# Four norm pieces over twelve tiles, and one rotated sum ahead of a power, in an AdaLN block with two local-attention layers

## The reference, cut to what matters

```python
x = states                                  # (4, 1024, 256), float32
sa, ca, ga, sb, cb, gb = modulation(c)      # six rows of 256 for each of 4 batches
h = layernorm(x) * (1 + ca) + sa
x = x + ga * attention(h)
h = layernorm(x) * (1 + cb) + sb            # this norm, of the last batch, is what the change cuts up
x = x + gb * ffn(h)                         # two layers, below

def layer(h):
    t = shift_token(h)                      # second half of the columns from the row before
    q, k, v = split(t @ wqkv)               # 8 heads of 64
    q, k = rotary(l2norm(q) * qs, l2norm(k) * ks)
    h = h + local_attention(q, k, v) @ wo   # window of 128, own block and the one before
    t = layernorm(shift_token(h)) * lg + lb
    a, g = split(t @ w1 + b1)
    return h + (a * gelu(g)) @ w2 + b2
```

## Time and profile before

| | us |
|---|---|
| median of 3 runs | 2335.64 |
| lowest and highest | 2334.77, 2335.74 |
| the profiled execution | 2336.77 |
| its span in the profile | 2335.0 |

### The profile page before, as it was taken

How to read it: one execution, slowest core, us unless ns; L and a number is a source line. 1 busy time by engine, 2 the same in 40 slices (tenths; PEclk the granted TensorE clock), 3 DMA queues, 4 the chain that set the end, 5 groups by cost and what they waited for, 6 DMA issues and landing times.

```text
span 2335.0 us, 61234 instructions
## 1 busy us (share of the span) xinstructions
PE 2249.1 (96%) x21120; PEld 1734.1 (74%) x21120; DVE 1918.6 (82%) x4512; ACT 1510.0 (65%) x2969; POOL 525.9 (23%) x637
## 2 busy tenths in 40 slices
PE   6999999999999999889999999999999999998999
PEld 4676777777777767567777777788777777776888
DVE  6999799979998999768888888567588888886776
ACT  5777577757776777447677766444476777765443
POOL 2000000000000000154555554012255555551000
PEclk9999999999999999989999999999999999999999
DMA  3100110001001100210000001000100000001110
GB/s 117 47 13 19 38 40 13 13 31 52 13 13 43 58 13 7 84 58 2 9 0 9 0 9 39 19 1 0 48 1 3 7 4 5 5 5 31 60 36 28
DMA packets 66987, 58.20 MB, mean 25 GB/s; under 512 B 4037, under 2 KB 64317, under 8 KB 66625
## 3 DMA queue, kind: packets, MB, share of 16 engines
q1 hardware_dynamic: 66880, 56.81, 7.9%
HBM read 44.21 MB, written 8.40 MB: 23 GB/s over the span
## 4 chain that ended last, share of the span: by engine, by line
PE 53%; DVE 2%; issue 1%; ACT 1%; POOL 0%; DVEq 0%; POOLq 0%; ACTq 0%
PE ly_ps L74 9%; PE ly_ps L75 9%; PE ly_ps L76 9%; PE ly_ps L1930 6%; PE ly_ps L1909 5%; PE ly_ps L1920 5%; PE ly_ps L1947 5%; PE ly_ps L1901 3%; PE ly_ps L1940 1%; PE ly_ps L1957 1%; PE ly_ps L1985 1%; PE ly_ps L1878 1%; DVE ly_masked L1598 1%; DVE ly_rope_t L1569 0%; DVE ly_rope_a L1566 0%
## 5 line engine op out<-in xcount | busy, mean ns | idle before, releaser
L610 ACT ACTIVATE at_p<-at_ps_s,at_shift 128x1024 f32<-128x1024 f32 (+3 forms) x384 | 335.5, 899 | 89.8 <-PE at_ps_s L814 48.9
L349 DVE TENSOR_TENSOR at_p_lo<-at_p,at_p_hi 128x1024 f16<-128x1024 f32 (+3 forms) x384 | 357.4, 952 | 5.5
L1371 ACT ACTIVATE ly_probs<-ly_masked,ly_small,ly_rq 128x256 f32<-128x256 f32 x512 | 301.6, 594 | 13.8 <-DVE ly_small L1601 13.8
L842 PE MATMUL at_ps_o<-at_v,at_p_hi 128*128 128x65 f16 x2304 | 238.0, 193 | 3.4 <-DVE at_p_lo L349 2.5
L842 PEld LDWEIGHTS at_ps_o<-at_v,at_p_hi 128*128 128x128 f16 x2304 | 210.6, 96 | 38.6 <-issue 25.8
L843 PE MATMUL at_ps_o<-at_v,at_p_hi 128*128 128x64 f16 x2304 | 237.1, 194 | 0.0
L1598 DVE CUSTOM_DVE_ANT_0 ly_masked<-ly_ps,ly_mask 128x256 f32<-128x256 f32 x512 | 196.1, 421 | 49.0 <-PE ly_ps L1909 36.6
L844 PE MATMUL at_ps_o<-at_v,at_p_lo 128*128 128x65 f16 x2304 | 236.0, 192 | 0.0
L1225 POOL TENSOR_TENSOR ly_rope_a<-ly_rope_a,ly_rope_t 128x512 f32<-128x512 f32 x128 | 164.2, 1283 | 318.5 <-DVE ly_rope_t L1569 318.5
L1379 ACT ACTIVATE ly_operands_plain<-ly_ps 128x512 f32<-128x512 f32 x256 | 153.3, 599 | 111.8 <-PE ly_ps L1920 103.9
L344 DVE CAST at_p_hi<-at_p 128x1024 f16<-128x1024 f32 (+3 forms) x384 | 206.8, 557 | 22.3 <-ACT at_p L610 13.5
(11 more groups left out here) (247 smaller groups left out, 6057.6 us busy)
## 6 DMA issues: line engine op xcount, KB each, us to landing
at_w_raw<-in_Wv SPq DMA_DIRECT2D x32, 128.0 KB, 2.3
at_w_raw<-in_Wq SPq DMA_DIRECT2D x32, 128.0 KB, 2.4
at_w_raw<-in_Wk SPq DMA_DIRECT2D x32, 128.0 KB, 2.4
at_xio<-in_states SPq DMA_DIRECT2D x4, 1024.0 KB, 6.7
ly_a_raw<-x SPq DMA_DIRECT2D x8, 512.0 KB, 4.4
out<-stream SPq DMA_DIRECT2D x16, 256.0 KB, 2.3
ly_shifted<-stream SPq DMA_DIRECT2D x8, 508.0 KB
x<-at_xio SPq DMA_DIRECT2D x3, 1024.0 KB, 4.4
```

The source lines that it names most:

```text
L349: dve.tensor_tensor(p_lo[u % P_RING][:, :, off:], probs[u % P_RING][:, :, off:], p_hi[u % P_RING][:, :, off:], ALU.subtract).then_inc(p_lo ...
L610: act.activation(probs[u % P_RING][:, :, off:], ps_s[u % 2][:, :, off:], ACT.Exp, bias=shift[:], scale=SCORE_SCALE).then_inc(exp_done, 1)
L842: pe.matmul(out, ph, ones_hi, start=(kt == 0 and t == 0), stop=False, skip_group_check=True)
L1371: step = act.activation(pr[:, j % 2, h, :], sm[:, j % 2, h, :], ACT.Exp, bias=small[:, j % 2, 1, h:h + 1], scale=rq[:, par, 2 * j + h:2 * ...
```

## The change

Two things change.

The norm of the last batch is done in four pieces of two tiles each (`piece(n)`), over tiles 0 to 11 of layer 0: statistics of piece n at the end of DVE's tile n (0 to 3), the variance and POOL's power at tile 4, the shift at tile 5, ACT's two instructions of a piece at the end of its tiles 6 to 9, the product of a piece (128x512) at the end of DVE's tiles 7 to 10, the sum of a piece at the end of DVE's tiles 8 to 11. For that the first twelve tiles of layer 0 (`HEAD = 12`) are straight code on DVE, ACT and POOL, and their loops run over tiles 12 to 27. PE's code, layer 1's loops and the DMAs stay.

And in front of tile 0 of both layers POOL sums the rotated queries (`add_rotated(l, 0, 0)`) ahead of the power for the query norms (`inverse_query_norms(l, 0, 0)`).

```diff
+NORM_PIECES = 4
+HEAD = 3 * NORM_PIECES
+
+def piece(n):
+    return range(n * TB // NORM_PIECES, (n + 1) * TB // NORM_PIECES)
...
# POOL, before tile 0 of layer 0 (and the same two lines of layer 1)
                         inverse_key_norms(l, 0)
+                        add_rotated(l, 0, 0)
                         inverse_query_norms(l, 0, 0, LP)
-                        add_rotated(l, 0, 0)
                         add_rotated(l, 0, 1)
...
-                    for t in range(V_RING):
+                    head = HEAD if l == 0 else V_RING
+                    for t in range(head):
                         tile(l, t, t % 2, (t + 3) % TB)
-                        if l == 0 and t == 0:
+                        if l == 0 and t == NORM_PIECES:
                             pool.wait_ge(n0_var, 1)
                             pool.tensor_tensor(col0[:, 2, :], col0[:, 1, :], expo[:], ALU.pow).then_inc(n0_rstd, 1)
                     if l == 0:
-                        pool.wait_ge(n0_done, 1)
+                        pool.wait_ge(n0_done, NORM_PIECES)
...
# ACT, at the end of its tile t
-                        if l == 0 and t == 1:
-                            act.wait_ge(n0_col, 1)
-                            act.wait_ge(keep["st_x1"], 16 * B)
-                            for i in range(TB):
+                        if l == 0 and NORM_PIECES + 1 < t < 2 * NORM_PIECES + 2:
+                            if t == NORM_PIECES + 2:
+                                act.wait_ge(n0_col, 1)
+                                act.wait_ge(keep["st_x1"], 16 * B)
+                            for i in piece(t - NORM_PIECES - 2):
                                 step = act.activation(x[:, NT - TB + i, :], x[:, NT - TB + i, :], ACT.Identity,
                                                       scale=col0[:, 2, i:i + 1], bias=col0[:, 3, i:i + 1])
                             step.then_inc(n0_xn, 1)
...
# DVE, at the end of its tile t
                         if l == 0:
-                            if t == 0:
-                                last_statistics()
+                            if t < NORM_PIECES:
+                                last_statistics(t)
+                            elif t == NORM_PIECES:
                                 last_variance()
-                            elif t == 1:
+                            elif t == NORM_PIECES + 1:
                                 last_shifts()
-                            elif t == 2:
-                                last_scale()
-                            else:
-                                last_offset()
+                            elif NORM_PIECES + 2 < t < 2 * NORM_PIECES + 3:
+                                last_scale(t - NORM_PIECES - 3)
+                            if t > 2 * NORM_PIECES - 1:
+                                last_offset(t - 2 * NORM_PIECES)
```

More of the change, by code:

```diff
@@ L1326, in _ @@
                     if l == 0:
-                        pool.wait_ge(n0_done, 1)
+                        pool.wait_ge(n0_done, NORM_PIECES)
                         pool.sem_inc(s["tick"], 1)
-                    with pool.Fori(V_RING // 2, NT // 2 - 2) as i:
+                    with pool.Fori(head // 2, NT // 2 - 2) as i:
                         for par in range(2):
@@ L1507, in _ @@
                             step.then_inc(n0_xn, 1)
-                    with act.Fori(V_RING // 2, NT // 2 - 2) as i:
+                    with act.Fori(head // 2, NT // 2 - 2) as i:
                         for par in range(2):
@@ L1521, in _, with last_statistics @@
                 start(dve, DVE_SEMS)
-                def last_statistics():
-                    for t in range(TB):
+                def last_statistics(n):
+                    for t in piece(n):
                         dve.bn_stats(st0[:, t, :], x[:, NT - TB + t, :]).then_inc(n0_bn, 1)
@@ L1533, in last_shifts, with last_scale, last_offset @@
                     dve.scalar_tensor_tensor(col0[:, 3, :], col0[:, 0, :], -0.5, col0[:, 2, :], ALU.mult, ALU.mult).then_inc(n0_col, 1)
-                def last_scale():
-                    dve.wait_ge(n0_xn, 1)
-                    dve.tensor_tensor(x[:, last, :], x[:, last, :], modB[:, B - 1, D:2 * D].unsqueeze(1).broadcast_to([P, TB, D]),
-                                      ALU.mult).then_inc(n0_scaled, 1)
-                def last_offset():
-                    dve.wait_ge(n0_scaled, 1)
-                    dve.tensor_tensor(x[:, last, :], x[:, last, :], modB[:, B - 1, 0:D].unsqueeze(1).broadcast_to([P, TB, D]),
+                def last_scale(n):
+                    tiles = slice(NT - TB + piece(n)[0], NT - TB + piece(n)[-1] + 1)
+                    dve.wait_ge(n0_xn, n + 1)
+                    dve.tensor_tensor(x[:, tiles, :], x[:, tiles, :],
+                                      modB[:, B - 1, D:2 * D].unsqueeze(1).broadcast_to([P, TB // NORM_PIECES, D]),
+                                      ALU.mult).then_inc(n0_scaled, 1)
+                def last_offset(n):
+                    tiles = slice(NT - TB + piece(n)[0], NT - TB + piece(n)[-1] + 1)
+                    dve.wait_ge(n0_scaled, n + 1)
+                    dve.tensor_tensor(x[:, tiles, :], x[:, tiles, :],
+                                      modB[:, B - 1, 0:D].unsqueeze(1).broadcast_to([P, TB // NORM_PIECES, D]),
                                       ALU.add).then_inc(n0_done, 1)
```

5 lines of the change are left out of this document (3 added, 2 removed).

## The result

| | runs | median us | lowest to highest |
|---|---|---|---|
| before | 6 | 2335.69 | 2334.77 to 2336.93 |
| changed | 6 | 2322.64 | 2317.76 to 2324.14 |

The changed kernel takes 0.994 of the time of the one before (95% interval 0.9927 to 0.9953): 13 to 14 us less, where 10.1 were forecast. The direction came out, and so did the two gains that the sum is made of; some 3 us came on top of them.

What follows compares the result with a forecast made beforehand. PE alone was taken to set the pace from tile 4 on. 9.66 us given back, less 0.5, plus 1.0, made 10.1 us, from the median of 2335.64 to 2325.5 us; range 2322.5 to 2329.8.

Steps and rivals of the forecast that it cites:

- The bound and the cover: Layer 0's tiles: PE alone sets the pace, the norm costs 9.66 us, DVE has 1.02 us to spare per tile.
- The two ways to find DVE's 1.02 us: DVE's margin from an undisturbed tile's keys' step, 1.02 us, and from tiles with the 128x2048 product, 1.03.
- Parts 1 to 3: Statistics (tiles 0 to 3), variance, power and shift (4 and 5), ACT (6 to 9): all hidden, no cost.
- Part 4: Products and sums, tiles 7 to 11: tiles 8, 9 and 10 each 0.18 us over, 0.5 us in all.
- Part 5: Rotated queries' sum ahead of their power: PE starts tile 0 0.97 us sooner; gain taken as 1.0 us.
- The sum: Whole kernel: 9.66 us given back, less 0.5, plus 1.0, is 10.1 us less, so 2325.5 us.
- nothing later can swallow it: Behind the change: PE goes on without waits through tiles 4 to 27, so the gain of 10.1 us stays.
- its term of the range: Range below rival 2's 2324.4 us: 1.0 us allowed for later slow-clock stretches that may shift.
- The thin cover: Rival, all twelve tiles: cover thinner than one tile shows, 0.4 us a tile, 2330.3 us; chance 0.12.
- The clock ahead of tile 0: Rival: PE's clock comes back sooner there and the earlier sum is worth 2.1 us, 2324.4 us; chance 0.13.
- The swap without effect: Rival, ahead of tile 0: the keys' sum or tile 1's norms hold PE instead, 2326.5 us; chance 0.10.
- The moved code: Rival, loops of both layers: instruction fetch at each pass costs 58 us, 2383 us; chance 0.03.

Runs made afterwards that it cites:

- two_pieces: The changed kernel with two norm pieces of four tiles in place of four of two; 2328.11 us in its one run.
- norm_only: The changed kernel with the queries' power ahead of the rotated sum again in both layers, four norm pieces kept; 2319.84 us median of 5, ratio 0.9938.
- before_again: The kernel before, unchanged, run and profiled a second time; 2336.28 us median of 11, ratio 1.0002.
- after_again: The changed kernel, unchanged, run and profiled a second time; 2322.19 us median of 5, ratio 0.9939 to the kernel before.
- before_pad2: The kernel before with two unneeded PE transposes ahead of each of six loop passes of layer 0; mean 2330.4 us, ratio 0.9981.

## Why the prediction was right, and where it was wrong

**The bound and the cover.** Right. PE paces the loop; the norm cost 9.66 us in four steps, and 9.09 came back, as the sum had it (9.66 less 0.5). The two ways to find DVE's 1.02 us were worth their lines: two_pieces puts it to a test at five more places.

**Parts 1 to 3.** Right: no step with statistics, variance, shift or ACT's work in it is over 14.03 us. ACT's two instructions were well inside: four cost only 0.1.

**Part 4.** Right, to a few hundredths: 14.17, 14.19 and 14.17 us behind tiles 8, 9 and 10, by PE's transposes of the stream, where 14.0 is usual, 0.5 in all. The pitch of 0.60 us holds, since DVE's product at 1138.96 is followed by the sum at 1139.56:

```profile
1138.96 0.68 DVE L1548 TENSOR_TENSOR stream<-stream,modB 128x512 f32<-128x512 f32 x1
1139.56 0.68 DVE L1555 TENSOR_TENSOR stream<-stream,modB 128x512 f32<-128x512 f32 x1
```

The duration that the Trainium skill (VectorE: DVE Perf Modes, the section on the TRN2 errata) gives for such an instruction, 0.69 us, is the 0.68 of these rows, but it isn't what a queue of them costs.

**Part 5.** Right in the trace: 3.03 us of wait for 4.03, the sum 0.18 us behind its releaser and 1.26 us long. The reason that the prediction gave for the shorter sum, DVE and POOL holding each other up, fits from the other side too: now DVE's product at 1001.25 takes 1.36 us while POOL sums. That the swap's microsecond reaches the end isn't shown: norm_only is as fast as the changed kernel. Ahead of layer 1 PE waits 1.38 us for DVE's sum, as before:

```profile
1661.08 0.66 PE L1917 MATMUL ly_ps<-ident,ly_rope_a 128*128 128x128 f32 x4 [1.38 <-DVE stream L1722]
```

**The sum.** The two terms together are 10.07 us in the traces, against 10.1 forecast; in the second pair of profiles (before_again and after_again) they are 1.70 and 9.16, so the 1.0 for the swap is good to some 0.7 us only. The step that failed is the one behind it: what lies behind the tiles was put at nothing ("nothing later can swallow it"), and its term of the range at 1.0 us, for slow-clock stretches that may shift. The profiles have 3.7 us less behind tile 28, where the change touches nothing: PE's waits in tiles 30 and 31 are as long as before, and the granted clock over tiles 28 to 31 is 1.00 for 0.92; the term of the range should have been 4 to 5. I read the stretches ahead of tile 0 closely, where a slow clock is cheap, and gave those at 1450, 1481, 2112 and 2143 us a lump of one, though windows over them would have shown them: the one at 1450 cost most of the 2.87 us of the fourth stretch and the one at 1481 the 0.86 of the fifth, and the pair near 2112 and 2143 fits the 4 to 5 us between the two groups of times.

**The rivals.** The thin cover: no. The clock ahead of tile 0: no, the stretch up to tile 0 is 0.98 us shorter in the first pair of profiles and 1.70 in the second, not 2.1. (By its own terms that price should have been 2.3: 0.97, and half of the 2.64 us by which the slow stretch was to shrink.) The swap without effect: in PE's wait no; in the time of the changed kernel none shows. The moved code: no; loops and straight code have the same steps. What came true wasn't on the list: with a gain in one place, PE's clock falls less often in a place far behind it.

**What stays open.** The falls come behind waits of PE in tiles 28 to 31 and in layer 1 that all these kernels have, and as long; the runs show that two transposes a pass can take them away and six bring them back. What decides in an execution whether the clock falls behind such a wait isn't shown. Nor is why the kernel before has the fall in tile 30 in both its profiles and its slower times in 73 of 85 runs. So I couldn't say for a given edit what the time will be, and of the 14 us only the 10 in the tiles are the change's own by a cause that was shown.

## What to carry to other kernels

To spread a lump of work that stalls the bounding engine, find the spare time of the helping engine per pass from one undisturbed pass, check it against one disturbed pass, and cut the pieces to fit; here that told the steps to about 0.1 us. Then list the stretches with a lowered clock over the whole span, also where the change touches nothing, and put their sum into the range, since a change far ahead of them can add or remove them. To know what a change of a few tenths of a per cent is worth by itself, add the same small useless work to both kernels in two or three sizes and compare the differences: one pair here said 14 us, the others 10, 7 and 15.

## What the runs showed that I had not expected

- Two useless transposes in each of PE's six passes, 1.0 us of its tile steps, made the kernel before 4.9 us faster (means 2330.4 and 2335.3).
- PE's wait in tile 30 was 1.93 or 1.94 us long with the clock's fall behind it and without.
- The times of a kernel fall into groups 4 to 5 us apart; in the two profiles of the kernel before they go with whether PE's clock falls near 2112 us (granted clock 0.89 or 1.00 over 45 us). Small additions close the gap (before_pad2: all 11 runs within 3.3 us).
- Keeping PE busy through a wait did keep its clock at 2.4 GHz (1.00 from 999 to 1006 us), and gained nothing, since POOL was next.
- A power of 128x8 on POOL took 2.10 us in place of 1.64 where DVE's product from SBUF (1.36 us in place of 0.69) stood beside it.
